# A 16-sequence transformer layer on one core: start-up loads and step 0 reordered, the attention norm folded into the residual on VectorE, K's low parts placed between LN3's moments

## The reference

```
x = x + layernorm(attention(layernorm(x)))        # q through rank 384, c = kv rank 128, k and v from c
x = x + layernorm(ffn(layernorm(x)))              # ffn: y = down(silu(gate) * up), then y / rms(y)
w = LUT[nibble(packed)] * scale                   # FFN weights, 4-bit
```

## Time and profile before

| what | value |
|---|---|
| time, median of 3 runs | 2572.87 us (2570.24 to 2573.47) |
| the profiled execution | 2573.7 us, its span 2571.7 us |
| mean granted TensorE clock | 0.983 |
| busy share of the span | PE 95%, weight loads 43%, DVE 59%, ACT 57%, POOL 26% |
| chain that ended last | PE 77%, SPq 7%, DVE 6%, ACT 5%, DMA 2%, POOL 2%, issue 2% |
| first maximum tile on PE (L492) in step 0, in step 1 | 77.2 us, 213.8 us |

### The profile page before, as it was taken

How to read it: one execution, slowest core, us unless ns; L and a number is a source line. 1 busy time by engine, 2 the same in 40 slices (tenths; PEclk the granted TensorE clock), 3 DMA queues, 4 the chain that set the end, 5 groups by cost and what they waited for, 6 DMA issues and landing times.

```text
span 2571.7 us, 38700 instructions
## 1 busy us (share of the span) xinstructions
PE 2440.2 (95%) x13372; PEld 1112.6 (43%) x13372; DVE 1524.9 (59%) x4210; ACT 1468.6 (57%) x3935; POOL 671.7 (26%) x711
## 2 busy tenths in 40 slices
PE   5579999999999999999999999999999999999978
PEld 2334444444444444444444444444444444444433
DVE  3857566564756666475565646656574665657442
ACT  2756647465574746557474665747566474756610
POOL 0431322313232231322213132322313222131322
PEclk9699999999999999999999999999999999999989
DMA  3212120201212011121201112030121202012000
GB/s 110 45 34 50 34 66 18 66 18 50 50 34 66 18 51 34 50 50 34 66 18 44 41 42 58 26 74 18 36 48 42 58 23 74 14 42 50 22 12 17
DMA packets 99558, 109.65 MB, mean 43 GB/s; under 512 B 22885, under 2 KB 73189, under 8 KB 99301
## 3 DMA queue, kind: packets, MB, share of 16 engines
q1 hardware_dynamic: 99362, 107.19, 15.9%
HBM read 39.24 MB, written 16.78 MB: 22 GB/s over the span
## 4 chain that ended last, share of the span: by engine, by line
PE 77%; SPq 7%; DVE 6%; ACT 5%; DMA 2%; POOL 2%; issue 2%; POOLq 0%; DVEq 0%
PE dense L325 56%; PE psO L525 6%; SPq L1159 5%; PE score L509 4%; PE low L492 3%; PE psO L325 3%; PE score L492 3%; SPq L1209 2%; DMA kst<-arena 1%; DVE st_ln L762 1%; ACT arena L704 1%; PE low L509 1%; ACT low L630 1%; ACT L636 1%; DVE low L985 1%
## 5 line engine op out<-in xcount | busy, mean ns | idle before, releaser
L325 PE MATMUL dense<-arena,wgu 128*128 128x512 f16 x4224 | 1002.0, 379 | 11.2 <-DVE late L862 10.3
L325 PEld LDWEIGHTS dense<-arena,wgu 128*128 128x128 f16 x4224 | 405.9, 97 | 446.8 <-DVE late L862 17.6
L325 PE MATMUL dense<-wdn,arena 128*128 128x512 f16 x2112 | 533.0, 380 | 2.6 <-POOL arena L1076 2.6
L1076 POOL TENSOR_TENSOR arena<-late,arena 128x512 f16<-128x512 f32 x176 | 203.6, 1157 | 1046.2 <-DVE arena L883 1046.2
L985 DVE CUSTOM_DVE_ANT_0 low<-low,mmax 128x128 f32<-128x128 f32 (+3 forms) x672 | 278.1, 434 | 264.2 <-PE low L492 260.9
L704 ACT ACTIVATE arena<-score 128x512 f32<-128x512 f32 (+3 forms) x720 | 302.2, 440 | 188.3 <-PE score L509 145.2
L630 ACT ACTIVATE low<-low,ncol 128x128 f32<-128x128 f32 (+3 forms) x672 | 300.3, 447 | 140.8 <-DVE ncol L985 133.0
L630 ACT ACTIVATE score<-score,ncol 128x384 f32<-128x384 f32 x352 | 214.2, 609 | 165.7 <-DVE ncol L985 164.9
L325 PEld LDWEIGHTS dense<-wdn,arena 128*128 128x128 f16 x2112 | 199.2, 98 | 186.7 <-issue 11.5
L985 DVE CUSTOM_DVE_ANT_0 score<-score,mmax 128x384 f32<-128x384 f32 x352 | 214.6, 648 | 103.1 <-PE score L492 102.4
L1089 POOL TENSOR_SCALAR_AFFINE_SELECT arena<-arena 128x512 f32<-128x512 f32 x240 | 163.9, 683 | 278.7 <-ACT arena L704 276.4
(11 more groups left out here) (135 smaller groups left out, 2947.5 us busy)
## 6 DMA issues: line engine op xcount, KB each, us to landing
qst<-arena SPq DMA_DIRECT2D x384, 64.0 KB, 2.1
kst<-arena SPq DMA_DIRECT2D x192, 128.0 KB, 2.6
xin<-x SPq DMA_DIRECT2D x16, 1024.0 KB, 5.2
late<-x SPq DMA_DIRECT2D x64, 256.0 KB, 2.8
out<-late SPq DMA_DIRECT2D x64, 256.0 KB, 2.0
qst<-mrow SPq DMA_DIRECT2D x96, 8.0 KB, 1.9
wgu<-wo_t SPq DMA_DIRECT2D x1, 1024.0 KB, 44.9
wgu<-wq_down SPq DMA_DIRECT2D x1, 768.0 KB, 7.2
```

The source lines that it names most:

```text
L325: ins = nc.tensor.matmul(dst, w, a, start=first and k == 0, stop=last and k == len(tt) - 1)
L1076: nc.gpsimd.tensor_tensor(ht[:, 1, m, :], tb[:, m % 2, :], ht[:, 0, m, :], ALU.subtract).then_inc(sem["hl"], 1)
```

## The change

It has three parts.

- **Loads.** SP issues wq_down and wq_up first, then x, the identity, the other raw weights, the gate/up codes and scales, wo, the down codes and scales, then small constants, and the bias rows last. Of the bias rows only 6 of 29 are loaded; DVE and GpSimd clear rows 96 to 127 of kst and qst first. PE's first products wait for wq alone, not for the constants.
- **Step 0.** `decode` is cut in two: the gate/up part stands ahead of wq's low parts, the down part behind the first low parts of x, ahead of C's. wo is converted earlier (ACT behind x's high parts, DVE behind K's low parts). Nine units instead of four come ahead of the slots, and the other 24 come 1.7 slots apart, up to slot 39. After unit 8 ACT makes the high part of every third unit (it was two of three) and DVE that of the others.
- **Steps 1 to 16.** One VectorE operation per tile, x1 = z * rstd + x1, replaces DVE's normalisation of z and GpSimd's addition; it leaves -mean * rstd out. LN3 is not changed by a constant per row; at the end `y_norm` subtracts mean2 * rstd2 with the output's own mean, for which it gets one more 128x1 operation. The wait for the residual's load moves from GpSimd to DVE. LN3's four moments and K's four low parts alternate.

```diff
@@ step 0: units and the engines that write them
-UNIT_SLOT = [-1] * 4 + [2 * k for k in range(UNITS - 4)]
+FIRST_UNITS = 9
+UNIT_SLOT = [-1] * FIRST_UNITS + [17 * k // 10 for k in range(UNITS - FIRST_UNITS)]
 RING = 3
+ACT_UNITS = [u for u in range(UNITS) if (u % RING < 2 if u < FIRST_UNITS else u % RING == 0)]
@@ block.tensor, prepare
-                pe.wait_ge(s_const, 64)
                 pe.wait_ge(s_wq, 32)
...
+                pe.wait_ge(s_id, 16)
@@ block.scalar, step: after the high parts of x
+                if isinstance(t, int) and t == 0:
+                    act.wait_ge(s_wo, 16)
+                    nc.scalar.activation(wo[:, 0, :, :], raw_wo, ACT.Copy, scale=S_W).then_inc(s_raw_hi, 1)
@@ block.vector, prepare
+                nc.vector.memset(kst[96:P, :, :], 0.0).then_inc(s_zero_k, 1)
...
+                decode(0)
                 for c in range(KC):
                     dve.wait_ge(s_prep_hi, c + 1)
@@ block.vector, y_norm
                     dve.wait_ge(sem["rs"], val("rs", t, n_y[0] + i + 1))
-                    normalise("lo", stage[:, i % 2, :], stage[:, i % 2, :], i).then_inc(sem["yn"], 1)
+                    q, rstd = ve["lo"][:, i:i + 1], rs["lo"][:, i:i + 1]
+                    link(t, nc.vector.scalar_tensor_tensor(q, mv["lo"][:, i, 0:1], rstd, ve["ln2"][:, i:i + 1],
+                                                           ALU.mult, ALU.add))
+                    linked(t)
+                    nc.vector.tensor_scalar(stage[:, i % 2, :], stage[:, i % 2, :], rstd, q,
+                                            ALU.mult, ALU.subtract).then_inc(sem["yn"], 1)
@@ block.vector, step
+                if isinstance(t, int) and t == 0:
+                    decode(1)
...
                 if ffn:
                     dve.wait_ge(sem["rs"], val("rs", t, 1))
+                    dve.wait_ge(sem["xres"], val("xres", t, 0))
                     for i in range(NT):
-                        normalise("ln2", z[:, i, :], z[:, i, :], i).then_inc(sem["z2"], 1)
+                        nc.vector.scalar_tensor_tensor(x1[:, i, :], z[:, i, :], rs["ln2"][:, i:i + 1], x1[:, i, :],
+                                                       ALU.mult, ALU.add).then_inc(sem["add2"], 1)
+                    link(t, nc.vector.tensor_tensor(ve["ln2"][:, :], mv["ln2"][:, :, 0], rs["ln2"][:, :], ALU.mult))
...
-                    for g in range(NG):
+                for g in range(NG):
+                    if ffn:
+                        dve.wait_ge(sem["add2"], val("add2", t, g + 1))
+                        link(t, nc.vector.bn_stats(st6["ln3"][:, g, :], x1[:, g, :]))
+                    if att:
                         low("K", g, qk[:, 3, g, :], S_QK / (S_C * S_W), qk[:, 2, g, :])
@@ block.gpsimd, step
                     power(t, "ln2", 1)
-                    pool.wait_ge(sem["xres"], val("xres", t, 0))
-                    for i in range(NT):
-                        pool.wait_ge(sem["z2"], val("z2", t, i + 1))
-                        nc.gpsimd.tensor_tensor(x1[:, i, :], x1[:, i, :], z[:, i, :], ALU.add).then_inc(sem["add2"], 1)
@@ block.gpsimd, ahead of everything
+            nc.gpsimd.memset(qst[96:P, :, :], 0.0).then_inc(s_zero_q, 1)
+            pool.wait_ge(s_zero_q, 1)
@@ block.sync
-            sp.dma_start(qst[96:P - 3, :, :], aug_q[0:HD - 3, :, :]).then_inc(s_aug, 16)
-            sp.dma_start(kst[96:P - 3, :, :], aug_k[0:HD - 3, :, :]).then_inc(s_aug, 16)
+            sp.wait_ge(s_zero_q, 1)
+            sp.wait_ge(s_zero_k, 1)
+            sp.dma_start(qst[96:96 + AUG, :, :], aug_q[0:AUG, :, :]).then_inc(s_aug, 16)
+            sp.dma_start(kst[96:96 + AUG, :, :], aug_k[0:AUG, :, :]).then_inc(s_aug, 16)
```

More of the change, by code:

```diff
@@ L101, in units_of, with act_units @@
     return [u for u in range(UNITS) if UNIT_SLOT[u] == slot]
+def act_units(u):
+    return sum(1 for n in ACT_UNITS if n <= u)
 def done(products):
@@ L762, in moments, with aggregate @@
                     link(t, nc.vector.bn_stats(st6[name][:, i, :], src(i)))
+                aggregate(t, name, tiles)
+            def aggregate(t, name, tiles):
                 linked(t)
@@ L790, in prepare, with decode_wo @@
                                                    ALU.mult, ALU.subtract).then_inc(s_prep_lo, 1)
-            def decode():
+            def decode_wo():
                 dve.wait_ge(s_raw_hi, 4)
@@ L797, in decode @@
                                                ALU.mult, ALU.subtract).then_inc(s_raw_lo, 1)
[L799 removed]
+            def decode(part):
                 ts = nc.vector.tensor_scalar
[L801 to L815 removed]
@@ L816, in decode @@
-                ts(sc32, sc16, FP8_SCALE * S_W4, None, ALU.mult).then_inc(s_bits, 1)
+                lo, hi = ((0, GUW), (GUW, W))[part]
+                sc_lo, sc_hi = ((0, 2 * MI * GROUPS), (2 * MI * GROUPS, NSC))[part]
+                n_bits = 7 * part
+                words, low3 = packed[:, lo:hi], bits1[:, 0:hi - lo]
+                sign = bits2[:, 0:hi - lo] if part == 0 else packed[:, 0:hi - lo]
+                dve.wait_ge((s_gu, s_dn)[part], 32)
+                if part:
+                    dve.wait_ge(s_bits, n_bits)
@@ new lines, in decode @@
+                ts(low3, words, 0x07070707, 2, ALU.bitwise_and, ALU.logical_shift_left).then_inc(s_bits, 1)
+                ts(sign, words, 0x08080808, 4, ALU.bitwise_and, ALU.logical_shift_left).then_inc(s_bits, 1)
+                dve.wait_ge(s_bits, n_bits + 2)
+                nc.vector.tensor_tensor(codes[:, 0, lo:hi], low3, sign, ALU.bitwise_or).then_inc(s_bits, 1)
+                dve.wait_ge(s_bits, n_bits + 3)
+                ts(low3, words, 0x70707070, 2, ALU.bitwise_and, ALU.logical_shift_right).then_inc(s_bits, 1)
@@ L818, in unit @@
+                ts(sign, words, -0x7F7F7F80, None, ALU.bitwise_and).then_inc(s_bits, 1)
+                dve.wait_ge(s_bits, n_bits + 5)
+                nc.vector.tensor_tensor(codes[:, 1, lo:hi], low3, sign, ALU.bitwise_or).then_inc(s_bits, 1)
+                ts(sc32[:, sc_lo:sc_hi], sc16[:, sc_lo:sc_hi], FP8_SCALE * S_W4, None, ALU.mult).then_inc(s_bits, 1)
             def unit(u):
                 bank_ = dense[u % RING][:, :].rearrange("p (a b) -> p a b", a=4)
-                if u % RING == 2:
+                if u in ACT_UNITS:
+                    dve.wait_ge(s_prep_hi, KC + act_units(u))
+                else:
@@ L942, in step @@
                         low("Q", g, qk[:, 1, g, :], HD ** -0.5 * S_QK / (S_X * S_WQ), qk[:, 0, g, :])
[L943 removed]
+                for g in range(NG):
[3 more added lines that the diff above has]
+                    if att:
                         low("K", g, qk[:, 3, g, :], S_QK / (S_C * S_W), qk[:, 2, g, :])
                 if ffn:
[L947 to L948 removed]
+                    aggregate(t, "ln3", range(NT))
                     ask_rstd("ln3")
                 if att:
+                    if isinstance(t, int) and t == 0:
+                        decode_wo()
                     for g in range(2, NG):
@@ L971, in step @@
                 if isinstance(t, int) and t == 0:
-                    decode()
                     for u in units_of(-1):
@@ L988, in step @@
                                                        accum_out=ncol[:, k:k + 1]).then_inc(sem["low"], 1)
-                    if isinstance(t, int) and t == 0:
+                    if isinstance(t, int) and t == 0 and slot:
                         for u in units_of(slot - 1):
-                            if u >= 4:
-                                unit(u)
+                            unit(u)
                     for part in range(2):
```

57 lines of the change are left out of this document (22 added, 35 removed), and 4 rows, old and new, of the table COUNTS.

## The result

The changed kernel takes 2550.59 us (median of 4 runs, 2549.71 to 2551.46) beside 2571.55 us for the kernel before on the same chip (4 runs, 2569.41 to 2573.47). The ratio is 0.9919, with a 95% interval of 0.9901 to 0.9936: 21.0 us faster. The forecast was 2556.3, a gain of 16.6. The profiled execution took 2549.71, its span is 2547.8.

What follows compares the result with a forecast made beforehand. PE bounds steps 1 to 15; step 0's SP queue is stuck behind bias rows on one DMA engine. Terms -16.6 + 4.1 + 1.5 - 5.6 + 1.5 - 1.7 + 0.2 = -16.6 give 2556.3 us, range 2547 to 2567.

Steps and rivals of the forecast that it cites:

- The head: Step 0 up to DVE's first reduction: at 62.3 us instead of 78.93, -16.6, bounds -20 and -11.
- the clock's fall: Step 0's C job: after idling 8 us PE may run twelve products at 1.2 GHz, 5.5 us; +1.7 in the sum.
- The rival of gu_packed's small pieces: SP queue stays stuck, filled by 2816 small pieces rather than bias rows; total -7, 2566 us; chance 0.04.
- other way to the same place: Head: the nine units ahead of the slots also put DVE's first reduction at 62 us, like the stack copies.
- The slots of step 0: Step 0's slots: DVE bounds slots 0 to 22; terms +4.1, +1.5 and -5.6 for the three stretches.
- The +4.1: Slots 0 to 22: DVE's unit work grows from 10.3 to 14.5 us, +4.1 (2 to 5).
- Slots 23 to 40: Step 0: more unit work on DVE, partly offset by fewer waits for ACT's high parts, +1.5 (0 to 4).
- slots 41 to 63: Step 0: units go away, so GpSimd's triangle no longer stands behind their work, -5.6 (-3 to -8).
- Steps 1 to 15: Later steps: PE is the bound; the new norm operation at 0.65 us per tile wins nothing, as DVE then waits.
- The term of +1.5: Steps 1 to 15: PE's third Q job 0.35 us late, absorbed in 11 steps, paid in four; 0 to +5.
- Step 16: Last step: LN2 and LN3 chain ends sooner, -1.7; the output norm's extra operation at the very end, +0.2.
- the price without a hold-up from GpSimd: Step 16: new operation at 0.65 us per tile, term -1.7; at 0.95 it would be -0.5.

Runs made afterwards that it cites:

- e1: Kernel before, bias rows of qst and kst loaded as 32 rows in one DMA each at the old place; 2564.68 us, ratio 0.9976.
- e8: Changed kernel with all 29 bias rows loaded, still last in the queue; 2559.27 us, ratio 0.9955.
- e5: Changed kernel with the units spaced and shared as before, four ahead of the slots; 2553.72 us, ratio 0.9935.
- e4: Changed kernel with the gate/up decoding behind x's low parts and the down decoding just ahead of the units; 2543.58 us, ratio 0.9897.
- e7: Changed kernel with the edits of e4, e3 and e6 together; 2542.7 us, ratio 0.9888.
- e9: Changed kernel with the 24 later units two slots apart instead of 1.7; 2550.01 us, ratio 0.991.
- e6: Changed kernel with ACT writing two of three high parts in all units, spacing kept; 2551.62 us, ratio 0.9922.
- e10: e7 with the later units two slots apart; 2539.6 us, ratio 0.9874.
- e2: Changed kernel with steps 1 to 16 as before, including the old norm of z and GpSimd's addition; 2550.87 us, ratio 0.9922.
- e3: Changed kernel with K's four low parts ahead of LN3's four moments again; 2549.38 us, ratio 0.992.

## Why the prediction was right, and where not

**The head: right, in mechanism and size** (-17.8 for -16.6). Read step by step: PE's first products at 7.73 (8.3), the decoding over at 25.5 (26.5), C's job at 30.37 (31.8) behind a wait of 8.51 (over 8), the clock's fall there (5.19 us for a forecast of 5.5), the stack copy at 42.20 (43), the first reduction at 61.10 (62.3). Each is about 1 us early. The weights had landed in time, so the decoding waited for nothing but DVE: the norm of x ended at 16.96 instead of 17.4, and low parts in a row came every 0.60 us, where the sum took 0.69 and 0.65. e1 and e8 show the cause from both sides: 32 rows in the old place free the queue, 29 rows in the new place come late and hold up the K copies. The rival of gu_packed's small pieces falls with e1 as the cause of the 59.77: they stand in the old place there, hold the next issue for 11.94 us at a full DMA share, and the stack copy leaves on time. The "other way to the same place", the nine units, comes out level with the first, as forecast; e5 with four has the same 61.16, so it costs 0.4 us at most. The clock's fall is right for this kernel, with a wait of 8 us; after a wait of 2 us it is open from one execution to the next (e4 and e7).

**The slots of step 0: mechanism right, the single sizes off.** In slots 0 to 22 the prediction says of DVE "it is the bound", and the table under e9 bears that out: the length follows DVE's busy time. The +4.1 was six operations at 0.69; DVE's busy time rose by 3.3 (31.6 to 35.0), since an operation behind another costs its pitch of about 0.6 and not its duration, and the stretch by 3.0. What the prediction does not price is what e6 met: work taken from DVE and given to ACT comes back as a wait when ACT's table loads stand ahead of it. No run varies the high parts alone at a place without that stop; e9 and e10 come nearest. Slots 23 to 40 paid +2.7 for +1.5 and slots 41 to 63 gave -7.6 for -5.6, both inside the bounds that were given; e5 shows that both come from where the units stand. The three terms came to 0.0 in the forecast and to -1.9 in the traces; their errors are -1.1, +1.2 and -2.0, so the first two cancel by luck.

**Steps 1 to 15: right that nothing is won.** The new operation has the price that was taken (0.65 to 0.7 per tile: 2.73 for four), and what it frees ends in an idle gap of 1.18 us. The third Q job starts 10.62 us behind C's job instead of 10.36, 0.26 late for a forecast of 0.35, and PE's wait for the K stack shrinks from 5.8 to 2.5 us: 3.3 of 15 x 0.26 = 3.9 us absorbed. The term of +1.5 was too high, since the absorbing was nearly complete; measured -0.5, which is nothing. e2 says the same of the whole edit, e3 of the alternation.

**Step 16: right for the part that was reasoned.** LN2's and LN3's part on DVE ends 1.7 us sooner, for PE's wait behind it is 10.88 where it was this before:

```profile
2467.63 0.69 PE L420 MATMUL low<-id,arena 128*128 128x128 f32 x2 [12.57 <-DVE arena L770]
```

That is as by the price without a hold-up from GpSimd (2.74 for four tiles); at 0.95 per tile it would have been 0.5. The old operation shows the hold-up too: four tiles took 1.91 us with GpSimd idle and 3.80 with its additions beside them. Behind it comes -1.9 us that the forecast did not have, in PE's clock. Windows from the transposes on, of the changed kernel (one row), and of the kernel before (two):

```profile
2445.00:2452.00 7.00, 5.25 (x25) 4.08 (x26) 4.33 (x8) 2.07 (x4) 0.00 (x0) 0.75 0.00 0
```

```profile
2467.00:2474.00 7.00, 5.43 (x21) 3.94 (x22) 4.40 (x8) 2.06 (x4) 0.00 (x0) 0.50 0.00 0
2474.00:2482.00 8.00, 8.00 (x33) 3.35 (x32) 1.80 (x3) 0.60 (x1) 1.02 (x1) 0.84 0.01 2
```

Both begin at 1.2 GHz; the changed kernel is back at 2.4 GHz within its window, the one before only in the next. This is not a property of the change: the stretch from the transposes to the end takes about 102 us or about 104 in nearly all profiled executions (102 in e1, e3, e4, e6 and e8, 104 in e2, e5, e7 and e10; 100.6 in e9), without a rule that the edits explain. So of the 24.0 us between the profiled spans 1.9 belong to it, and the medians, 21.0 apart, are the better measure of the change.

In sum: the head gave 1.2 us more than forecast, the slots 1.9, the later steps 2.0, the last step's chain 0.2 and its clock 2.1; that is -24.0 for -16.6. No single step carries the difference.

## What to carry to other kernels

A queue whose one issue takes many us is stuck on a transfer ahead of it, not on its own: look at the DMA share in that window, and when it is near 1/16, look for a transfer with a count of rows like 29 (32 rows did no such thing here); at a share near 1 a long issue is only a full load, as gu_scales' 7.20 us. When such a stop is removed, ask at once which engine's order of work was written around it, because most of the gain lies in moving that work (5 to 6 us for the queue, 12 for the move, and 7 more by e4 for one that had been moved too far forward). And where an engine is busy for nine tenths of a stage and taking work from it does not shorten the stage, look which wait took the place of the work before ruling the engine out: here it was 2.99 us behind two table loads of the engine that got the work.
